# A message-passing kernel on one core: twenty gathered places a tile instead of sixteen, slots unpacked in threes, loops written out

## What is computed

```python
def _step(embedding, src, dst, etype, W_msg, b_msg, w_ih, w_hh, b_ih, b_hh):
    n = embedding.shape[0]
    m = (embedding @ W_msg.T + b_msg).reshape(n, N_EDGE_TYPES, DIM)
    q = m[src, etype]
    r = jax.ops.segment_sum(q, dst, num_segments=n)
    return _gru_cell(r, embedding, w_ih, w_hh, b_ih, b_hh)
...
for _ in range(4):
    embedding = _step(embedding, src, dst, etype, W_msg, b_msg, w_ih, w_hh, b_ih, b_hh)
```

## Time and profile before

| | |
|---|---|
| median of 3 runs | 2250.77 us (2250.59 to 2251.88) |
| profiled execution | 2250.78 us |
| its span | 2248.9 us |
| mean granted clock of TensorE | 0.928 |
| TensorE busy | 2064.0 us, 92% |
| TensorE weight loads | 1443.1 us, 64% |
| VectorE busy | 1346.0 us, 60% |
| ScalarE busy | 495.3 us, 22% |
| GpSimd busy | 885.8 us, 39% |

### The profile page before, as it was taken

The page is one execution under the profiler, slowest core; times in us unless marked ns, Lnnn a source line. Parts: engine busy times, 40 slices in busy tenths (PEclk is TensorE's granted clock), DMA queues, the critical chain, the costliest instruction groups (busy, mean ns, idle before and its releaser), DMA issues.

```text
span 2248.9 us, 42235 instructions
## 1 busy us (share of the span) xinstructions
PE 2064.0 (92%) x15410; PEld 1443.1 (64%) x16017; DVE 1346.0 (60%) x2875; ACT 495.3 (22%) x1130; POOL 885.8 (39%) x1022
## 2 busy tenths in 40 slices
PE   3666665899999999999899999999999999999998
PEld 2333333899989988898655576555765557655576
DVE  8999998777777778786842236422354223553233
ACT  4989887200000000000210002100022000220001
POOL 4978773000000000000058860488604886048870
PEclk9555555899999999999999999999999999999999
DMA  2000000000000000002431111311103111033111
GB/s 83 24 35 35 24 35 36 30 1 2 1 2 2 2 1 2 1 1 91 145 93 42 42 34 40 99 41 42 36 23 113 41 43 37 24 112 70 41 39 31
DMA packets 62730, 89.73 MB, mean 40 GB/s; under 512 B 31953, under 2 KB 48927, under 8 KB 59654
## 3 DMA queue, kind: packets, MB, share of 16 engines
q1 hardware_dynamic: 21185, 54.88, 7.4%
q0 software_dynamic: 38400, 31.28, 6.0%
q10 hardware_dynamic: 2944, 0.93, 0.2%
HBM read 47.48 MB, written 39.05 MB: 38 GB/s over the span
## 4 chain that ended last, share of the span: by engine, by line
PE 75%; DVE 16%; issue 4%; DVEq 3%; ACT 2%; POOL 0%; POOLq 0%; DMA 0%; ACTq 0%
PE ps L912 39%; PE ps L1016 28%; PE ps L895 4%; DVE marks L1218 3%; DVEq L1205 2%; DVE m_full L1688 2%; DVE m_parts L1681 2%; DVE weighed L1223 1%; PE ps L926 1%; DVE dig L1246 1%; DVE big L1248 1%; PE ps L875 1%; PE ps L837 1%; PE ps L1001 1%; DVE hot_pair L1220 1%
## 5 line engine op out<-in xcount | busy, mean ns | idle before, releaser
L508 POOL DMA_INDIRECT big<-messages_by_edge_kind,edge_row x480 | 616.6, 1285 | 1156.7 <-issue 876.2
L912 PE MATMUL ps<-slots,m_parts 125*128 125x436 fp8e4 (+1 forms) x5600 | 960.8, 330 | 4.5 <-DVE m_parts L1681 3.2
L912 PEld LDWEIGHTS ps<-slots,m_parts 125*128 125x128 f16 x5600 | 539.9, 98 | 360.6
L1016 PE MATMUL ps<-parts,big 125*128 125x256 f16 x6125 | 669.0, 273 | 1.1 <-DVEq L1630 1.1
L1016 PEld LDWEIGHTS ps<-parts,big 125*128 125x128 fp8e4 x6125 | 590.7, 98 | 64.1
L1519 DVE TENSOR_SCALAR slots<-big 128x1400 int32<-128x1400 int32 (+1 forms) x224 | 196.5, 920 | 259.5 <-PE ps L912 241.3
L793 PE MATMUL ps<-hot_pair,weighed 125*128 125x228 f16 x1000 | 219.5, 372 | 118.4 <-ACT weighed L621 73.1
L793 PEld LDWEIGHTS ps<-hot_pair,weighed 125*128 125x128 f16 x1000 | 118.0, 124 | 219.8 <-ACT weighed L621 181.3
L621 ACT ACTIVATE weighed<-marks,win_w 125x128 f16<-125x128 f16 x625 | 194.5, 390 | 40.7 <-DVE marks L1218 40.7
L560 ACT ACTIVATE rs<-rs 125x25 f32<-125x25 f32 (+3 forms) x5 | 1.1, 216 | 697.5 <-DVE rs L1088 697.5
L1708 DVE SCALAR_TENSOR_TENSOR gate_r<-ps,over,gate_r 128x436 f32<-128x436 f32 (+2 forms) x32 | 20.0, 624 | 213.6 <-PE ps L895 169.6
(11 more groups left out here) (231 smaller groups left out, 1553.2 us busy)
## 6 DMA issues: line engine op xcount, KB each, us to landing
messages_by_edge_kind<-m_parts SPq DMA_DIRECT2D x20, 1120.0 KB
packed_counts<-packed SPq DMA_DIRECT2D x16, 625.0 KB, 2.9
big<-messages_by_edge_kind,edge_row POOLq DMA_INDIRECT x480
big<-packed_counts SPq DMA_DIRECT2D x4, 1400.0 KB, 6.4
big<-packed_counts SPq DMA_DIRECT2D x3, 1050.0 KB, 5.8
messages_by_edge_kind<-m_parts SPq DMA_DIRECT2D x20, 130.0 KB
hd<-in_x SPq DMA_DIRECT2D x1, 1562.5 KB
x_again<-in_x SPq DMA_DIRECT2D x1, 1562.5 KB
```

The costliest lines, as they stand in the source:

```text
L508: pool.indirect_dma_start(out=picked[0:CH, r, w, :, :].rearrange("p h f -> p (h f)"), out_offset=None, in_=m_dram[:, :], in_offset=bass.In ...
L912: last = pe.matmul(ps[:, k % 2, 0:SIZES[k] * QD], m_parts[0:Q, a, t, h, :], slots_f8[0:Q, t % 2, 0:SIZES[k], a, 0:QD], start=a == 0 and t ...
L1016: last = pe.matmul(ps[:, n % RING, 0:2 * F], tot_f8[0:Q, c, a, :], both((parts0, parts1)[par], a), start=a == 0, stop=a == TILES - 1)
```

## The change

Three things change together.

1. *Picked places.* QD falls from 109 to 105, so twenty places of each tile are picked. No windows of places are formed any more: the last 133 x 128 = 17024 edges of the sorted list are gathered, 128 rows at a time, 133 gathers a step. Each gather's targets lie within PC = 40 columns that start at a base fixed in advance (BASES), so a gather is two matmuls of 40 columns into one bank of 500 sums, which a matmul with zeros clears first. There are 27 lots; LOTS_AT is written anew. Edges that belong to dense places, or fall outside their 40 columns, have no column; an edge outside its columns sends all engines to the general path. The rows and targets come from three loads on ScalarE's queue behind its first `block_of`, and VectorE works them out in `late_edges`, placed behind the one-hots of the last counted places; GpSimd's staging and VectorE's `edge_parts` go. `mark_targets` runs in seven pieces and one hop earlier. SyncE's last store is split into (20, 23) and (23, 25).
2. *Unpacking.* The instructions of a slot cover three tiles and the rest: 75 and 25 rows for four tiles, 75 rows in one instruction for three.
3. *Order on VectorE.* The loops of hops and of steps are written out, and the sums of the picked turn (`sum_low`, `sum_high`) stand behind dense turn 5's update instead of ahead of it.

```diff
-QD = 109
+QD = 105
...
-GW = 15
-PC = 2 * TILES
-PAIRS = (Q - QD) // 2
+GE = 128
+GATHERS = 133
+FIRST_EDGE = E - GATHERS * GE
+PC = 40
+PICKED = TILES * (Q - QD)
+BASE_STEP = 8
+BASE_ROWS = (GATHERS + BASE_STEP - 1) // BASE_STEP
+BASE_AT = PICKED - (128 * GATHERS - 64) // 33 - PC // 2
+BASES = [min(max(BASE_AT + 31 * (j // BASE_STEP) + 4 * (j % BASE_STEP), 0), PICKED - PC) for j in range(GATHERS)]
+MARKED = 21
...
-LOTS = PAIRS * GW // LOT
+LOTS = (GATHERS + LOT - 1) // LOT
+LOT_SIZE = [min(LOT, GATHERS - LOT * lot) for lot in range(LOTS)]
...
-LOTS_AT = {(1, 0): (0, 1), (1, 1): (2,), (1, 2): (3,), (1, 3): (4, 5), (2, 0): (6,), (2, 1): (7,), (2, 2): (8, 9), (2, 3): (10,),
-           (3, 0): (11, 12), (3, 1): (13,), (3, 2): (14,), (3, 3): (15,), (4, 0): (16, 17), (4, 1): (18,), (4, 3): (19, 20),
-           (5, 0): (21,), (5, 1): (22,), (5, 2): (23,)}
+LOTS_AT = {(1, 0): (0, 1), (1, 1): (2,), (1, 2): (3, 4), (1, 3): (5,), (2, 0): (6, 7), (2, 1): (8,), (2, 2): (9,), (2, 3): (10,), (3, 0): (11, 12), (3, 1): (13,), (3, 2): (14,), (3, 3): (15, 16), (4, 0): (17,), (4, 1): (18,), (4, 2): (19,), (4, 3): (20,), (5, 0): (21,), (5, 1): (22,), (5, 2): (23,), (5, 3): (24,), (6, 0): (25, 26)}
...
-STORED = [(0, 5), (5, 10), (10, 15), (15, 20), (20, 25)]
+STORED = [(0, 5), (5, 10), (10, 15), (15, 20), (20, 23), (23, 25)]
...
             block_of(0, 0, BQ, None)
+            with nc.allow_non_contiguous_dma("last edges, 128 at a time"):
+                for to, a in ((late_target, dst), (edge_row[:, :], src), (late_type, edge_type)):
+                    act.dma_start(to, a[FIRST_EDGE:E].rearrange("(j p) -> p j", p=GE)).then_inc(s_late, 16)
...
+                if lot == 0:
+                    pe.matmul(ps[:, 6, 0:PICKED], zeros[:, :], hot_room[:, 0:PICKED].bitcast(F8), start=True, stop=False, skip_group_check=True)
+                for w in range(LOT_SIZE[lot]):
+                    at = lot * LOT + w
                     for h in range(2):
-                        last = pe.matmul(ps[:, 6, pair * PC:(pair + 1) * PC], picked[0:CH, r, w, h, :], hot_to_f8[0:CH, pair, first + w, :],
-                                         start=first + w == 0 and h == 0, stop=first + w == GW - 1 and h == 1, skip_group_check=True)
+                        last = pe.matmul(ps[:, 6, BASES[at]:BASES[at] + PC], picked[:, r, w, h, :], hot_to_f8[:, at, :],
+                                         start=False, stop=at == GATHERS - 1 and h == 1, skip_group_check=True)
...
+            def late_edges():
+
+                at = slice(0, GATHERS)
+                rel, base, low, high = late_rel[:, at], late_base[:, at], late_low[:, at], late_high[:, at]
+                dve.wait_ge(s_late, 48)
+                step(TS(base, base, 0.0, float(PICKED - PC), ALU.max, ALU.min))
+                step(TS(rel, late_target, -float(TILES * QD), None, ALU.add))
+                step(TT(win_to[:, :], rel, base, ALU.subtract))
...
+                STT(out=edge_row[:, :], in0=edge_row[:, :], scalar=float(TYPES), in1=late_type, op0=ALU.mult, op1=ALU.add).then_inc(s_rows, 1)
...
                 onehots(q, q % DEPTH, q % WINDOWS)
+            late_edges()
             sum_digits(NB - 2, 0)
...
-                for lo, hi in ((0, size // 2), (size // 2, size)):
+                for lo, hi in ((0, 3), (3, size))[:size - 2]:
...
-                with dve.Fori(0, HOPS // 2 - 2) as i:
-                    steps.loop(i, 2 * (1 + 5 * TILES))
-                    for par in range(2):
-                        hop(2 * i + par, par, TILES * (2 * i + par))
-                steps.done(HOPS // 2 - 2)
-                for h, beside in ((HOPS - 4, scales_beside), (HOPS - 3, edges_beside), (HOPS - 2, targets_beside)):
+                    if c % 3 == 2 and c // 3 * MARKED < GATHERS:
+                        mark_targets(c // 3)
+
+                for h in range(HOPS - 4):
+                    hop(h, h % 2, TILES * h)
+                for h, beside in ((HOPS - 4, scales_beside), (HOPS - 3, targets_beside), (HOPS - 2, None)):
...
                         if not last:
-                            if after[0] == "picked":
-                                sum_low(turn + 1, picked_sums(after[1]), picked_parts(after[1], u + 1, 1), picked_parts(after[1], u + 1, 0))
                             unpack(s, i + 1, 1)
...
                     dve.sem_inc(s_emb, 1)
+                    if after and after[0] == "picked":
+                        sum_low(turn + 1, picked_sums(after[1]), picked_parts(after[1], u + 1, 1), picked_parts(after[1], u + 1, 0))
...
-                with dve.Fori(0, STEPS - 1) as s:
-                    steps.loop(s, 4 * TURNS)
-                    gnn_step(s, True)
-                steps.done(STEPS - 1)
-                gnn_step(STEPS - 1, False)
+                for s in range(STEPS):
+                    gnn_step(s, s < STEPS - 1)
```

## The result

The changed kernel takes 2346.6 us against 2251.0 before, a ratio of 1.043 (1.041 to 1.045). It is slower by 4.3% where a gain of 0.9% was forecast. Its profiled execution has a span of 2342.8 us, 93.9 more than before. Two places hold nearly all of it, and the prediction put both at nothing.

The account below looks back on a forecast made before the run. TensorE was taken as the bound, nearly full in hops and gathering. From 2250.78 us, terms -30.9 + 3.6 + 5.8 + 4.4 - 2.2 - 1.8 = -21.1 gave 2229.7 us; forecast 2224 to 2236, range 2221 to 2246.

Parts of the forecast that it names:

- Gathers: GpSimd's 133 gathers a step, at a pace of 1.51 to 1.54 us, come in time: cost nothing, bound 0 to +3.
- rival (a): Picked rows come late, TensorE waits before the last lots; gain gone at pace 1.60, 2279 us at 1.65; chance 0.16.
- Rival (c): The last edges' 4-byte loads arrive late and counting waits: 2430 us at 100 pieces a us; chance 0.04.
- The last edges' loads: Counting stage: three loads on ScalarE's queue, ready before VectorE needs them at 369 us; with their arithmetic 0, give or take 1.
- Dense columns: TensorE's dense gathering: fewer columns make pieces of 9.0 and 6.8 us, 7.73 us less a step, -30.9 us in four.
- Unpacking: VectorE's 75-row unpack takes 2.3 us; TensorE waits +5.8 us after the messages and +4.4 us between steps.
- Rival (b): Unpacks over odd rows run at the full rate of an even count: 2222 to 2238 us; chance 0.08.
- Loops: VectorE's step loops written out: 0.74 us less for each of three steps, -2.2 us; nothing gained in the hops.
- Picked matmuls: TensorE: 266 instead of 240 a step at 27 ns each, plus a clearing matmul: +0.91 a step, +3.6 us.
- The picked sums: Moved behind dense turn 5's update, they are ready about when TensorE reaches the picked gates: 0, up to +1.5 a step.
- rival (d): The picked sums are late by over 1 us a step: 2234 to 2238 us; chance 0.05.

Follow-up runs that it names:

- the paced runs: 128-row gathers with a scratch fill on GpSimd behind each: 2254.8 us in the kernel before; 2229.9 in the changed kernel with loads on SyncE's queue and halves at three places.
- the last version: Changed kernel with 128-row gathers, a longer scratch fill (384 elements) behind each, loads on SyncE's queue, halves at three places: 2222.4 us, ratio 0.987.

## Why the prediction was wrong, point by point

**Gathers: the step that failed first.** It asked one question, whether rows come in time, and bounded the cost at 0 to +3 a step. No row had a gather of 128 rows, so its price was taken from 125, and the doubtful side was taken to be the slow one: rival (a) lost time only above a pace of 1.557 us. The gather came out faster, 0.944 us, and the pace within a run 1.25. The rows were early, and the early pace itself cost TensorE 60.5 us of gaps and a clock at its lower level behind the longer ones, some 93 us in place of nothing. What a faster gather would set off was not asked. The chance of "slower", 0.17, came from rivals (a) and (c), and neither is what made it slower. The Trainium skill, "DMA: Bandwidth & Descriptors", section "Why a DMA increments its semaphore by 16 and not by 1", has a shape of 128 partitions use 16 DMA engines, and in general the largest divisor up to 16, which makes five of 125. The packets a gather, 32 against 80, agree that the shapes are split differently. It says nothing of another engine's issue, and the paced runs show that the split alone is harmless.

**The last edges' loads: the step that failed second.** The prediction compared the loads' end with VectorE's need at 369 us and put the term at 0, give or take 1. It did not name what is queued behind a load on the engine that issues it, though the earlier trace rows showed pieces moving at 483 a us, some 35 us for one load of 17024 by that row. The second and third load held ScalarE's queue for 20.8 us, ScalarE had 19.9 us of idle time, and the hops began 18.4 us late. Rival (c) was late data; VectorE never waited for them.

**Right, with their sizes.** Dense columns: pieces of 9.00 and 6.79 us, as worked out. Unpacking: 2.34 us for 75 rows (2.3 taken), TensorE's wait behind the messages 1.8 us, and +10.1 in the run with that edit alone (+10.2). Rival (b) is out. The rule of the Trainium skill, "VectorE: DVE Perf Modes", section "What auto-detection actually checks", takes the two-port mode where the outermost counts of source and destination are both even or equal; with both sides counting 75 that would be some 1.2 us, which no run shows, and the 2.34 us fit it if the unbroken destination counts as 2100. Loops: steps of 283.21 us (283.22). Picked matmuls: 0.53 us for 20 of 40 columns, as 0.54 for 20 of 50, so the 27 ns was not the columns, and the upper value was the right one. The picked sums: TensorE waited once, 0.5 us, as it did before, so rival (d) did not come. A step of 283.22 - 7.73 + 0.91 - 0.46 = 275.9, the prediction's terms without those for the unpacking, stands against 276.07 in the last version. With the unpacking's 1.45 + 1.45 the terms make 278.8, not the 278.5 that the prediction wrote; the version with 125 rows and SyncE's loads has 279.2 in the one step whose boundary kept the full clock.

**Missed, but small.** With odd rows at the step boundary TensorE stands idle twice there, 1.1 and 2.1 us, where it was once, 1.87. The 1.3 us more lie within the bounds given (0.85 to 1.45). But in the run with 125 rows and SyncE's loads the granted clock fell behind that at two of the three boundaries, and those two steps are 280.9 us against 279.2, another 1.7 us each, which the term did not hold:

```profile
1386.00:1396.00 10.00, 7.92 (x33) 4.18 (x38) 7.50 (x14) 4.71 (x9) 0.00 (x0) 0.83 0.39 128
1666.00:1676.00 10.00, 7.35 (x38) 4.33 (x45) 8.78 (x16) 5.14 (x9) 0.00 (x0) 1.00 0.40 130
```

(The table by stretches, around the first and the second boundary; the granted clock is the third column from the end, 0.83 and 1.00.)

**Rival (a) was real, in another kernel.** With 125 rows and unpacking in halves the mean pace was 1.587 us, and TensorE waited 29 us for lots, 7.3 a step, where that run's expectation had 5 to 9: the mechanism as described, but not in the changed kernel.

## What to carry to other kernels

Ask of every part that a change makes faster what it will do to the others, as of every part that it makes slower: here a GpSimd gather that took 0.94 in place of 1.21 us cost TensorE some 93 us, and in the kernel before with 128 rows a fill that slowed the gathers to one every 1.51 us took back 107 us (2362.2 to 2254.8). Loads of thousands of short pieces, issued one right behind another, held the queue that issued them; spread them out, or give them to an engine that has nothing behind them. When two losses are in a change, taking away one can show nothing, since the other may move; take away both before judging either.

## What the runs showed of the hardware that was not expected

- An indirect gather on GpSimd of 128 rows takes 0.944 us, of 121 1.026, of 120 0.982, of 119 1.102 and of 125 1.209: more rows can take less time.
- Runs of gathers started every 1.25 to 1.41 us leave TensorE with 41 to 78 us of gaps in these four steps; in the longest ones of the changed kernel single instructions come 0.70 us apart or a multiple of it. At 1.51 us there are 0 to 4.5 us of gaps, and at 1.55 none. Half the bytes do not make them fewer (70.9).
- The second and third of three loads of 17024 four-byte pieces, issued right behind each other, hold the issuing queue 10.4 us each over 128 partitions, and of 17000 pieces over 125 partitions 20.4 and 20.3. The same loads of 17024 pieces 22 us apart on another queue take 0.44 us each.
